# Residual additions, layer norm and node projection of the mixture moved into one block, in three groups of tiles

## The reference

```
x  = x + gnn0(layernorm(x)) + linear_attention0(layernorm(x))
# the mixture: eight experts, the best two per node
xn = layernorm(x)
rw, re = top_k(softmax(xn @ router.T), 2);  rw = rw / rw.sum(-1)
x  = x + xn + sum over the two chosen e of rw_e * (gelu(xn @ w1[e] + b1[e]) @ w2[e] + b2[e])
# layer 1
xn  = layernorm(x)                                   # (x - mean) / sqrt(var + 1e-5)
hid = relu((xn[src] + edge_attr) @ W1 + b1)          # 40000 edges
agg = segment_sum(hid @ W2 + b2, dst)
x   = x + xn + agg + linear_attention1(xn)
x   = x + one_of_eight_experts(layernorm(x))
```

## Time and profile before

| | us |
|---|---|
| median of 3 runs | 1331.4 (1331.01 to 1337.01) |
| the profiled execution, own time | 1334.28 |
| its span in the trace | 1332.3 |
| TensorE busy | 1123.4 (84%) |
| VectorE busy | 662.3 (50%) |
| ScalarE busy | 440.5 (33%) |
| GpSimd busy | 485.2 (36%) |
| mean granted clock of TensorE | 0.937 of full speed |

### The profile page before, as it was taken

The page is one execution under the profiler, slowest core; times in us unless marked ns, Lnnn a source line. Parts: engine busy times, 40 slices in busy tenths (PEclk is TensorE's granted clock), DMA queues, the critical chain, the costliest instruction groups (busy, mean ns, idle before and its releaser), DMA issues. The chain is left out here.

```text
span 1332.3 us, 21998 instructions
## 1 busy us (share of the span) xinstructions
PE 1123.4 (84%) x7698; PEld 907.6 (68%) x7698; DVE 662.3 (50%) x1616; ACT 440.5 (33%) x923; POOL 485.2 (36%) x530
## 2 busy tenths in 40 slices
PE   2888898998538884379999999999999799938997
PEld 2688897466427773268788888888876645527886
DVE  5777731678664323735454555554375512152332
ACT  2477710522315441113243333333333242321110
POOL 3000000103026773027766666666574000004442
PEclk9899999998859997589999999999999889968998
DMA  6000000500352334556566666666573094386551
GB/s 134 1 2 2 2 2 16 109 4 1 102 172 90 101 100 116 140 162 197 183 192 184 186 190 186 190 190 179 161 220 105 14 305 105 82 201 211 180 182 38
DMA packets 97268, 164.52 MB, mean 123 GB/s; under 512 B 15633, under 2 KB 59309, under 8 KB 96901
## 3 DMA queue, kind: packets, MB, share of 16 engines
q1 hardware_dynamic: 71669, 89.65, 23.4%
q0 software_dynamic: 25488, 73.39, 18.9%
HBM read 137.36 MB, written 27.63 MB: 124 GB/s over the span
## 5 line engine op out<-in xcount | busy, mean ns | idle before, releaser
L2357 POOL DMA_INDIRECT em_gathered<-edge_table,el_which x313 | 301.4, 963 | 131.2 <-issue 74.8
L2369 PE MATMUL em_projected<-em_w,em_attr 128*128 128x256 f32 x1252 | 281.3, 382 | 7.6 <-PEq L1988 7.6
L2369 PEld LDWEIGHTS em_projected<-em_w,em_attr 128*128 128x128 f32 x1252 | 238.8, 191 | 42.3 <-issue 9.9
L2447 DVE TENSOR_TENSOR em_hidden<-em_projected,em_gathered 128x512 f32<-128x512 f32 (+1 forms) x157 | 108.2, 689 | 204.0 <-PE em_projected L2369 125.1
L2469 ACT ACTIVATE em_hidden<-em_hidden 128x512 f32<-128x512 f32 (+1 forms) x157 | 98.7, 628 | 270.2 <-DVE em_hidden L2447 269.6
L2869 PE MATMUL oe_banks<-oe_wd,xn_T 128*128 x432 | 99.1, 384 | 0.0
L2783 POOL DMA_INDIRECT oe_hidden<-oe_table,oo_node x27 | 25.9, 960 | 182.1 <-DMA oe_table<-state 131.3
L2869 PEld LDWEIGHTS oe_banks<-oe_wd,xn_T 128*128 128x128 f32 x432 | 81.3, 193 | 10.2
L2812 PE MATMUL oe_banks<-xn_T,oe_w 128*128 128x500 f32 x160 | 71.1, 596 | 1.8 <-DMA oe_b<-in_ffn_b_T 1.8
L663 ACT ACTIVATE nm_adj_T<-nm_banks 125x500 f16<-125x500 f32 x100 | 60.0, 603 | 23.0 <-PE nm_banks L566 19.9
L1380 POOL IOTA el_up_i<- 20x40 int32 x1 | 0.2, 161 | 180.1 <-POOLq L741 180.1
(11 more groups left out here) (502 smaller groups left out, 2218.9 us busy)
## 6 DMA issues: line engine op xcount, KB each, us to landing
em_attr<-in_edge_attr_sets SPq DMA_DIRECT2D x156, 256.0 KB, 3.5
oe_table<-state SPq DMA_DIRECT2D x20, 448.0 KB
oe_wd<-in_ffn_Wd SPq DMA_DIRECT2D x8, 1024.0 KB
em_gathered<-edge_table,el_which POOLq DMA_INDIRECT x313, 3.6
mx_w<-in_ffn_w SPq DMA_DIRECT2D x16, 256.0 KB
oe_table<-state SPq DMA_DIRECT2D x1, 2248.8 KB
state<-in_x SPq DMA_DIRECT2D x5, 448.0 KB
state<-in_x SPq DMA_DIRECT2D x1, 2240.0 KB
```

The lines of the kernel that those rows point to most:

```text
L2357: nc.gpsimd.indirect_dma_start(out=gathered[:, n % GATHERED, :], out_offset=None, in_=table, in_offset=bass.IndirectOffsetOnAxis(ap=lanes. ...
L2369: last = nc.tensor.matmul(projected[:, k % BANKS, n % 2, :], attr[:, k % ATTR_RING, (n % 2 * KB + f) * 128:(n % 2 * KB + f + 1) * 128], w1 ...
L2447: nc.vector.tensor_tensor(pair_slots(k), projected[:, k % BANKS, 0:width, :], gathered[:, at:at + width, :], ALU.add).then_inc(pre_ready, 1)
```

## The change

The block of `normalise_to_first` is gone and its work is done inside the block of `mixture`:

- The 20 tiles form three groups, of 8, 8 and 4 tiles. VectorE adds the answers of group g and, between the additions of each tile, normalises the tiles of group g - 1 (one per tile in the second group, two per tile in the third). Variance, Sqrt and inverse root are done once per group.
- The bias is added by TensorE, as a third matmul with one row of ones, instead of by VectorE. ScalarE copies both the turned tiles and the projected rows out of PSUM, in this order: the copy of turned tile t - 1, then of projected rows t - 3, the last ones at the group's end; then the Sqrt of the next group.
- The eight attribute loads and the loads of `EdgeWeights` are issued in `mixture` right behind the expert weights, and belong to `EdgeInputs`, made before `mixture`. The table's stores are issued there too, and the wait for them moves from the end of a block to GpSimd, ahead of its first gather in `edge_messages`. The clearing of semaphores moves to the start of `edge_messages`.
- To make room, buffers share memory: the ring of gathered rows and the hidden tiles lie in the second answer's buffer, the one-hot rows and values of `Origins` in `w1_now` and `rows_T`, and the projected rows waiting for their store in the expert weights.

```diff
@@ Origins.__init__
+        lent = lambda a, size: a.bitcast(BF16)[:P, 0:size]
+        self.hot_row = (sb(...) if hot_row is None else lent(hot_row, ...).rearrange(...))
+        self.values = (sb(...) if values is None else lent(values, ...).rearrange(...))
@@ mixture: buffers
-        second = sb("answer", [P, TILES, DIM])
-        rows = sb("rows", [128, RING, DIM])
-        hidden_T = sb("hidden_T", [128, KEPT, 2 * KB * 128])
+        second_all = sb("answer", [128, TILES, DIM])
+        second = second_all[:P]
+        rows = second_all[:, 0:RING, :]
+        hidden_T = second_all[:, RING:RING + 2 * KEPT, :].rearrange("p (j u) d -> p j (u d)", u=2)
+        GROUPS, BANKS = ((0, 2), (2, 4), (4, CHUNKS)), 4
+        tiles_in = lambda g: range(4 * GROUPS[g][0], 4 * GROUPS[g][1])
+        norm_turned, projected = banks[:, 0:BANKS], banks[:P, BANKS:2 * BANKS]
@@ mixture: SyncE
                 clear(sp, done)
+                for k in range(ATTR_RING):
+                    load_attributes(sp, A, edge.attr, edge.attr_loaded, k)
+                edge.weights.sync(sp)
...
+                for q in range(CHUNKS):
+                    sp.wait_ge(kept, 4 * (q + 1))
+                    load_rows(sp, edge.table[q * CHUNK:(q + 1) * CHUNK, :].rearrange("(t p) d -> p t d", p=P), staged(q), edge.stored)
@@ mixture: TensorE
+                def turn_rows(t):
+                    pe.wait_ge(normed, t + 1)
+                    if t >= BANKS:
+                        pe.wait_ge(copied, t - BANKS + 1)
+                    for k in range(KB):
+                        last = nc.tensor.transpose(norm_turned[:, t % BANKS, k * P:(k + 1) * P], xn[:, t, k * 128:(k + 1) * 128], c.ident[:P, :P])
+                    last.then_inc(transposed, 1)
+
+                def project(t):
+                    pe.wait_ge(copied, t + 1)
+                    if t >= BANKS:
+                        pe.wait_ge(kept, t - BANKS + 1)
+                    for k in range(KB):
+                        nc.tensor.matmul(projected[:, t % BANKS, 0:DIM], xn_T[:, k, t * P:(t + 1) * P], first_w[:, k, :],
+                                         start=(k == 0), stop=False)
+                    nc.tensor.matmul(projected[:, t % BANKS, 0:DIM], c.ones[0:1, 0:P], first_b[0:1, :],
+                                     start=False, stop=True).then_inc(ready, 1)
+                for g in range(len(GROUPS)):
+                    for t in tiles_in(g):
+                        turn_rows(t)
+                        if t - 2 in tiles_in(g):
+                            project(t - 2)
+                    for t in tiles_in(g)[-2:]:
+                        project(t)
@@ mixture: ScalarE
+                def keep_turned(t):
+                    act.wait_ge(transposed, t + 1)
+                    nc.scalar.activation(xn_T[:, :, t * P:(t + 1) * P], norm_turned[...], ACT.Copy).then_inc(copied, 1)
+                def keep_rows(t):
+                    act.wait_ge(ready, t + 1)
+                    nc.scalar.activation(staged(t // 4)[:, t % 4, :], projected[:, t % BANKS, 0:DIM], ACT.Copy).then_inc(kept, 1)
+                for g in range(len(GROUPS)):
+                    mine = slice(tiles_in(g)[0], tiles_in(g)[-1] + 1)
+                    act.wait_ge(var_ready, g + 1)
+                    nc.scalar.activation(std[:, mine], var[:, mine], ACT.Sqrt).then_inc(std_ready, 1)
+                    for t in tiles_in(g):
+                        if t - 1 in tiles_in(g):
+                            keep_turned(t - 1)
+                        if t - 3 in tiles_in(g):
+                            keep_rows(t - 3)
+                    keep_turned(tiles_in(g)[-1])
+                    for t in tiles_in(g)[-3:]:
+                        keep_rows(t)
@@ mixture: VectorE (find_var, find_root, normalise: as in the removed block, on the tiles of one group)
-                for t in range(TILES):
-                    (two additions of tile t, then measure(t - 1))
+                for g in range(len(GROUPS)):
+                    for n, t in enumerate(tiles_in(g)):
+                        add_answers(t)
+                        if t - 1 in tiles_in(g):
+                            measure(t - 1)
+                        if g and n == 0:
+                            find_root(g - 1)
+                        if g:
+                            each = len(tiles_in(g - 1)) // len(tiles_in(g))
+                            for u in tiles_in(g - 1)[n * each:(n + 1) * each]:
+                                normalise(u)
+                    measure(tiles_in(g)[-1])
+                    find_var(g)
+                find_root(len(GROUPS) - 1)
+                for t in tiles_in(len(GROUPS) - 1):
+                    normalise(t)
@@ normalise_to_first: removed
@@ edge_messages
             def _(sp):
+                clear(sp, done)
             def _(pool):
                 nc.gpsimd.iota(order_i[:], ...)
+                pool.wait_ge(edge.stored, 32 * CHUNKS)
                 for n in range(BLOCKS):
```

More of the change, by code:

```diff
@@ L1704, in tensor_steps, with mixture @@
         last.then_inc(self.found, 1)
-def mixture(p, c, A, state, x, xn, xn_T, first_w, first_b):
+def mixture(p, c, A, state, x, xn, xn_T, first_w, first_b, edge):
     nc = p.nc
@@ L2307, in scalar, with edge_messages @@
             nc.scalar.activation(self.std[:], self.var[:], ACT.Sqrt).then_inc(self.std_ready, 1)
-def edge_messages(p, c, A, lanes, w1, attr, attr_loaded, table, hidden_sum, attention):
+def edge_messages(p, c, A, lanes, w1, edge, hidden_sum, attention, done):
     nc = p.nc
     GATHERED, HIDDEN_RING, BANKS = 12, 2, 3
+    attr, attr_loaded = edge.attr, edge.attr_loaded
     pairs_of = lambda s: range(s * SET_PAIRS, min((s + 1) * SET_PAIRS, PAIRS))
@@ L2357, in _ @@
                     nc.gpsimd.indirect_dma_start(
-                        out=gathered[:, n % GATHERED, :], out_offset=None, in_=table, in_offset=bass.IndirectOffsetOnAxis(
+                        out=gathered[:, n % GATHERED, :], out_offset=None, in_=edge.table, in_offset=bass.IndirectOffsetOnAxis(
                             ap=lanes.which[:, n:n + 1].bitcast(mybir.dt.uint32), axis=0)).then_inc(got[n % GATHERED], 16)
@@ L2662, in sync, with __init__, layer1 @@
         sp.dma_start(self.gamma[:], A["mix1_gamma"].partition_broadcast(P)).then_inc(self.loaded, 16)
[L2665 to L2667 removed]
+class EdgeInputs:
+    def __init__(self, p, A, scope):
+        self.table = p.nc.dram_tensor("edge_table", [NODES, DIM], F32).ap()
+        self.attr = p.sb("em_attr", [128, ATTR_RING, 2 * DIM], scope=scope)
+        self.attr_loaded = [p.sem(f"em_attr_loaded{u}", False) for u in range(ATTR_RING)]
+        self.stored, self.weights = p.sem("em_stored", False), EdgeWeights(p, A, scope)
+def layer1(p, c, A, x, xn, xn_T, lanes, in_degree, w1, edge):
     done = p.retire()
+    w = edge.weights
     with ExitStack() as scope:
         hidden_sum = p.sb("hidden_sum", [P, TILES, DIM], scope=scope)
[L2671 removed]
         with ExitStack() as edges:
[L2673 to L2675 removed]
+            attention = Attention(p, c, x, xn, xn_T, in_degree, w, edges)
+            edge_messages(p, c, A, lanes, w1, edge, hidden_sum, attention, done)
             p.reuse(done)
[L2677 to L2679 removed]
+        general_messages(p, c, A, lanes, w1, edge.table, hidden_sum)
         node_messages(p, c, x, hidden_sum, w)
@@ L3064, in graph_layers @@
         first_b = p.sb("em_b1", [P, DIM], scope=graph)
-        mixture(p, c, A, state, x, xn, xn_T, first_w, first_b)
+        edge = EdgeInputs(p, A, graph)
+        mixture(p, c, A, state, x, xn, xn_T, first_w, first_b, edge)
     if upto >= 3:
-        layer1(p, c, A, x, xn, xn_T, lanes, in_degree, first_w, first_b)
+        layer1(p, c, A, x, xn, xn_T, lanes, in_degree, first_w, edge)
 def laid_out(i):
```

147 lines of the change are left out of this document (41 added, 106 removed).

## The result

The kernel after takes 1369.97 us (median of 4 runs, 1369.38 to 1370.11), the kernel before in the same runs 1331.67. The ratio is 1.0278, 95% interval 1.0251 to 1.0304: **slower by 38 us**, where 1330.5 was forecast and 1336.0 was the upper end.

The account below looks back on a forecast made before the run. TensorE was taken to set the time from the edge messages on, whose start the first gather decides. Gather 1.05 us earlier, preloads 0.2 later: 1331.4 - 0.85 = 1330.5 us, range 1321.5 to 1336.0.

Parts of the forecast that it names:

- TensorE's cost of a tile: Projection: 1.08 us per tile plus 0.43 for the bias matmul (0.2 to 0.6), so 1.51 at high clock, 3.0 at low.
- group 0: First eight tiles on TensorE: clock low at 540.1, rising at 548.15 after 4.75 us of work, projected by 557.4.
- the third rival: Projection: the clock stays high over both pauses between groups, 2.4 us earlier, 1328.1; chance 0.14.
- TensorE's first norm transpose: Start of normalising on TensorE: at 540.1 instead of 555.57.
- The emptying at each group's end: Between groups: Sqrt stands behind the last projected rows' copy, so engines empty in turn, 2.1 us each time.
- the first rival: Projection: the engines never empty between groups, everything 8.4 us earlier, 1322.1; chance 0.15.
- The clock's fall behind a pause: Projection: TensorE's clock falls after each pause between groups, costing 2.0 us, then 0.4 (bounds 0 and 3.4 each).
- Behind the projection: From projection's end at 583.9 to edge messages: TensorE starts at 585.65, first gather at 587.3, 1.05 us earlier than before.
- TensorE's lead: Edge messages: TensorE starts 2.0 us earlier, but loses this at ScalarE's copy of attention keys, at 599.08 before.
- The sum: Whole kernel: span 1332.3 - 1.05 + 0.2 = 1331.45 us; median 1331.4 - 0.85 = 1330.5 us.
- The second, the preloads: Mixture: attribute and weight loads delay the experts, giving 1333.0 to 1336.6 us, middle 1334.8; chance 0.13.
- The fourth: ScalarE between groups: tables reloaded for the second and third groups' Sqrt, 2 x 1.28 = 2.6 us, 1333.1; chance 0.05.

Follow-up runs that it names:

- full rows: Changed kernel with the bias matmul as identity times 125 bias rows instead of one row of ones times one bias row: 1333.36 us, ratio 1.0001.
- full rows and early Sqrt: Changed kernel with identity times 125 bias rows, and the next group's Sqrt ahead of the last three copies of projected rows: ratio 0.9924, again 0.9927 (1416.23 us).
- 125 rows of ones: Changed kernel with the bias matmul fed by 125 rows of ones and 125 bias rows instead of one each: ratio 0.9990.
- the early Sqrt: Changed kernel, one-row bias kept, with the next group's Sqrt ahead of the last three copies of projected rows: 1346.1 us, ratio 1.0124.
- the fifty matmuls ahead: Changed kernel, one-row bias and Sqrt where it was, with fifty full matmuls of no use ahead of the first group: ratio 1.0261.

## Why the prediction was wrong

**The step that failed** is TensorE's cost of a tile: the bias matmul was priced "by the nearest row, two of the four records beside it", 0.43 at the high clock, and group 0 was built on a clock that is "low at 540.1" and rises after 4.75 us of work, "to 548.15". The 0.43 is right for a matmul with 96 rows or more: with full rows the tile is 1.51 at the high clock and the bias is worth 8.7 us by the medians, both as forecast. With one row the tile is 0.77 longer at the high clock (1.85 less 1.08), beyond the upper end of 0.6. That alone would be 7 us. The rest is what no term held: the row of 5.5 us at the low clock was carried over from a stream of full matmuls to one in which two records of eight have one row, and there the clock does not rise, or late. Per tile 1.95 us more than at the high clock, 1.49 of them for the clock (3.0 less 1.51, the full-row tile at either level) and 0.46 for the pair. By the traces of the one-row and the full-row kernel the projection takes 77.2 instead of 42.9, 34.3 more; with 1.3 by which it begins later in that execution, the first gather is 35.6 later, and the span 35.2 longer. The first edge matmuls are slower too (5.39 us for 16 instead of 3.69), but TensorE then waits for ScalarE's copy in both (2.45 and 2.26 us), so that this adds nothing. The two ratios differ by 0.0277, or 36.9 us.

The prediction had written that the one-row matmul "is not in the trace in this form", and bounded its time. It did not bound what it does to its neighbours. The clock was weighed only as a matter of pauses (the third rival). Two of its sums don't come out, though nothing hangs on them: 551.6 plus 4.1 is 555.7 and not 555.9, and the bounds that it names for clock and bias give 1325.3 to 1336.9, not 1327.5 to 1333.5.

**What held**, against the kernel with full rows:
- TensorE's first norm transpose 25.6 us behind the last expert matmul: measured 26.0, and 25.6 with full rows.
- The emptying at each group's end, Sqrt right behind the copy: 2.1 forecast, 1.86 and 1.82 measured. Without them (full rows and early Sqrt, against 125 rows of ones on the same chip) 8.3 us are won, 1424.52 to 1416.23; the first rival had 8.4 for it.
- The clock's fall behind a pause: with full rows one of 3.4 us in the second group, which costs half of that, 1.7 (2.0 taken); behind the second pause none in the projection (0.4 taken), the next fall began at 602.1, in the edge messages.
- Behind the projection: TensorE's edge start 1.75 after its end, measured 1.78; the gather 3.4 after, measured 4.09 (`2.09 <-DMA edge_table`, the wait for the last stored rows), so 0.7 too little. TensorE's lead is lost at ScalarE's copy, as said: 2.45 us of waiting at 637.70.
- The sum: with the bias matmul as it was priced the kernel is 0.85 us faster by the forecast; measured 0.2 us faster (1333.36 against 1333.57), its interval reaching from 1.7 us faster to 1.9 slower. The rest of the sum held. The traces say the same if one counts from the end of the last expert matmul, since that end itself moves by up to 4.4 us from trace to trace: to the first gather it is 73.8 us before, 72.8 by the forecast and 72.6 with full rows (517.95 to 590.55), against 107.3 with one row.

**The rivals.** The first (never empty) is false for this kernel and right as a repair. The second, the preloads: from the first gather to the last expert matmul's end

```profile
394.28 1.02 POOL L1817 DMA_INDIRECT mx_answer<-mx_xn_rows,mo_node  x1 [37.97 <-DVE mo_node L1691]
...
516.10 2.76 PE L1862 MATMUL mx_banks<-mx_w,mx_answer 128*128 x12
```

are 124.6 us, and 124.6 in the kernel before (389.88 to 514.51). The 4.4 us by which both are later are there ahead of the first preload (377.58): 2.7 of them when the mixture begins, the whole 4.4 at TensorE's matmul that counts the chosen experts (370.93 instead of 366.56). With no bias matmul they are absent (first transposes at 540.6, forecast 540.1). With full rows the same stretch is 125.4 and with the early Sqrt 125.6, so the preloads cost 1 us at most. The third (clock high over both pauses) is false for the first pause and true for the second in the kernel with full rows; in the changed kernel the clock was low before both. The fourth: one table load, 1283 ns, in ScalarE's idle time at 517; the Sqrts among the copies load none. The 1283 ns are the figure of the Trainium skill (ScalarE: Activation LUTs, What ACT_TABLE_LOAD costs), and the rule on switches didn't bite, as no second load stands among the copies and Sqrts.

## What to carry to other kernels

A matmul that adds a bias from one row is not the smallest part of a stream but one that can hold TensorE at 1.2 GHz: give it all the rows there are (an identity times the bias rows costs no more instructions), or leave the addition to an engine with gaps. A price taken from the nearest row is one for that row's shape (0.43 was taken, 0.77 came); ask also what the new shape does to the clock and the weight loads of its neighbours, and bound that. And a wait behind which two engines empty is repaired by its place in the queue alone: the Sqrt three copies earlier was worth 8 us with the clock in order.

## What the runs showed of the hardware

- The 40 bias records: mean 707 ns with one row, 708 with 64, 418 with 96 and with 125; clock included. At the low clock a pair holds TensorE for 1.14 or 1.15 us with one or 64 rows and for 0.85 with 96 or 125. The step lies between 64 and 96 rows; where, was not tried.
- The clock, once low, stayed at 1.2 GHz through 69.5 us of unbroken work with two one-row records in eight, and through the whole projection with 64-row ones, and rose 2.9 to 3.5 us after the first edge matmul in these and in the changed kernel. With 96 or 125 rows it rose 5.2 to 9.2 us after the first transpose, with one or two bias pairs run at the low clock, and also in a stream with idle time in every tile; in the kernel before with full rows it rose after 3.2 us, as the first pair began.
- Where it rose between one-row matmuls (576.1 with the early Sqrt, 633.9 with the fifty matmuls ahead), 3.15 us without one had just passed, and then it held with them. At 554.50 in the kernel before with one row and at 607.92 in the changed kernel the same 3.15 us brought no rise. What decides that is open, and so is the one unprofiled run of four in the kernel before with one row that was 25 us shorter.
- A high clock that TensorE had before the first tiles (fifty matmuls) was low again within 1.7 us of the first tile's transposes, with full and with one-row bias alike.
- The same kernel before took 1333.57 on one chip and 1416.39, 1425.75 and 1426.13 on three others; no run shows why. The ratio of the repaired kernel was the same on two of these, 0.9924 and 0.9927; on the first chip it was not run.
